# Row-maximum passes over 1,024 keys instead of 512 in the second and third block of an attention kernel

## The reference, cut to what matters

```python
def _L0_xattn_ref(image_features, text_features, Wq, bq, Wk, bk, Wv, bv):
    query = jnp.einsum('bqi,ih->bqh', image_features, Wq) + bq
    key = jnp.einsum('bkt,th->bkh', text_features, Wk) + bk
    value = jnp.einsum('bkt,th->bkh', text_features, Wv) + bv
    scale = 1.0 / jnp.sqrt(jnp.asarray(HID, query.dtype))
    scores = jnp.einsum('bqh,bkh->bqk', query, key) * scale
    weights = jax.nn.softmax(scores, axis=-1)
    return jnp.einsum('bqk,bkh->bqh', weights, value)
...
x = x + jnp.tanh(g_xattn[0]) * _L0_xattn_ref(_layernorm(x, axis=-1), ctx_768, ...)
x = x + jnp.tanh(g_ffn[0]) * _L0_ffn_ref(_layernorm(x, axis=-1), ...)
```

## Time and profile before

| | us |
|---|---|
| median of 3 runs (303.92 to 305.04) | 304.34 |
| the profiled execution | 305.22 |
| its span, from the first to the last instruction | 303.1 |
| PE busy | 289.5 (96%) |
| DVE busy | 220.0 (73%) |
| ACT busy | 211.3 (70%) |
| POOL busy | 81.7 (27%) |

### The profile page before, as it was taken

How to read it: one execution, slowest core, us unless ns; L and a number is a source line. 1 busy time by engine, 2 the same in 40 slices (tenths; PEclk the granted TensorE clock), 3 DMA queues, 4 the chain that set the end, 5 groups by cost and what they waited for, 6 DMA issues and landing times.

```text
span 303.1 us, 4501 instructions
## 1 busy us (share of the span) xinstructions
PE 289.5 (96%) x1577; PEld 252.3 (83%) x1577; DVE 220.0 (73%) x395; ACT 211.3 (70%) x333; POOL 81.7 (27%) x81
## 2 busy tenths in 40 slices
PE   6798899999999999999999989899999999999995
PEld 5565699999999999998999979888878878888883
DVE  4589699998598987995347478855868956756666
ACT  2678656666575665657677757669879889888881
POOL 5999940000000300000002944433141311111310
PEclk9889799999999999999999999999999999999999
DMA  7500400000000000000000252221011121121120
GB/s 209 211 0 3 138 1 3 0 2 0 2 0 2 1 0 2 0 0 4 0 0 2 69 139 71 73 67 71 32 39 35 41 68 35 42 99 36 37 67 35
DMA packets 10641, 12.40 MB, mean 41 GB/s; under 512 B 1530, under 2 KB 6524, under 8 KB 10620
## 3 DMA queue, kind: packets, MB, share of 16 engines
q1 hardware_dynamic: 10140, 11.90, 12.9%
q10 hardware_dynamic: 480, 0.23, 0.3%
HBM read 11.57 MB, written 0.56 MB: 40 GB/s over the span
## 4 chain that ended last, share of the span: by engine, by line
PE 87%; DVE 7%; POOL 2%; issue 2%; ACT 1%; DMA 1%; DVEq 0%; POOLq 0%; ACTq 0%
PE ps L872 8%; PE ps L873 8%; PE ps L893 8%; PE ps L808 8%; PE ps L874 8%; PE ps L895 8%; PE ps L894 8%; PE ps L939 5%; PE ps L941 5%; PE ps L940 5%; PE ps L967 4%; PE ps L968 4%; PE ps L966 4%; DVE pmax L584 3%; POOL norm L361 1%
## 5 line engine op out<-in xcount | busy, mean ns | idle before, releaser
L532 ACT ACTIVATE ex_hi<-ps 128x768 fp32r<-128x768 f32 (+1 forms) x78 | 57.0, 731 | 62.7 <-PE ps L874 62.1
L697 DVE TENSOR_TENSOR ex_lo<-ps,ex_hi 128x768 fp32r<-128x768 f32 (+1 forms) x78 | 66.4, 852 | 29.0 <-ACT ps L533 27.4
L584 DVE TENSOR_REDUCE pmax<-ps 128x1 f32<-128x512 f32 (+1 forms) x104 | 65.8, 666 | 11.5 <-PE ps L808 10.3
L738 DVE TENSOR_TENSOR ex_lo<-ps,ex_hi 128x512 fp32r<-128x512 f32 x64 | 44.0, 691 | 29.8 <-ACT ps L548 29.2
L533 ACT ACTIVATE ps<-ps 128x768 f32<-128x768 f32 (+1 forms) x78 | 56.5, 724 | 0.0
L872 PE MATMUL ps<-q_hi,ctxT_hi 97*128 97x384 f32 (+1 forms) x153 | 50.1, 327 | 2.9 <-DVE ex_lo L697 2.4
L547 ACT ACTIVATE ex_hi<-ps,cols 128x512 fp32r<-128x512 f32 x64 | 44.2, 691 | 11.6 <-PE ps L941 10.8
L893 PE MATMUL ps<-ex_hi,ctx_hi 128*97 128x384 f32 (+1 forms) x153 | 49.6, 324 | 0.0
L873 PE MATMUL ps<-q_lo,ctxT_hi 96*128 96x384 f32 (+1 forms) x153 | 49.5, 324 | 0.0
L874 PE MATMUL ps<-q_hi,ctxT_lo 96*128 96x384 f32 (+1 forms) x153 | 49.1, 321 | 0.0
L895 PE MATMUL ps<-ex_lo,ctx_hi 128*97 128x384 f32 (+1 forms) x153 | 48.7, 318 | 0.0
(11 more groups left out here) (117 smaller groups left out, 443.8 us busy)
## 6 DMA issues: line engine op xcount, KB each, us to landing
w_raw<-in_L_ffn_W_dram SPq DMA_DIRECT2D x16, 256.0 KB, 3.1
r_b<-routing SPq DMA_DIRECT2D x16, 256.0 KB, 3.2
raw<-in_ctx_dram SPq DMA_DIRECT2D x6, 384.0 KB, 6.1
tok<-in_x_dram SPq DMA_DIRECT2D x1, 384.0 KB, 4.3
out_dram<-norm SPq DMA_DIRECT2D x1, 256.0 KB, 2.5
tok<-in_x_dram SPq DMA_DIRECT2D x1, 128.0 KB, 2.3
out_dram<-norm SPq DMA_DIRECT2D x1, 128.0 KB, 1.7
out_dram<-norm ACTq DMA_DIRECT2D x1, 128.0 KB, 1.8
```

What stands on the lines that cost most here:

```text
L532: nc.scalar.activation(ex_pair(ex_hi, u % P_RING, js, n), scores, ACT.Exp)
L584: nc.vector.tensor_reduce(pmax[:, FIRST_TILE[b] + t, place:place + 1], MPAIR[:, s % 2, 0:w], AX.X, ALU.max).then_inc(max_reduced, 1)
L697: nc.vector.tensor_tensor(ex_pair(ex_lo, u % P_RING, js, n), whole, ex_pair(ex_hi, u % P_RING, js, n).bitcast(F32), ALU.subtract).then_inc ...
```

## The change

In blocks 1 and 2 one pass covers 1,024 keys. It is made of two matmuls of 512 columns, which fill both banks of `MPAIR`, and one reduction of DVE that reads both banks. A block then has 21 passes in place of 39: 3 tiles by 6 pieces of 1,024 keys, and 3 passes of 260 keys. Since a pass takes both banks, it waits for the reduction of the pass right before it. Block 0's own passes stay as they are. `finish_max` reads the 7 columns of `pmax` that are filled.

```diff
+    PASS = [BANK] + [2 * BANK] * (NB - 1)
+    PLACES = [-(-NKEY // p) for p in PASS]
+    SLOTS = [[(t, w * p, min(p, NKEY - w * p), w) for w in range(-(-NKEY // p)) for t in range(n)]
+             for n, p in zip(BLOCK_TILES, PASS)]
...
+        def max_home(b, s):
+            return flat(MPAIR) if b else MPAIR[:, s % 2, :]
...
-                nc.vector.tensor_reduce(pmax[:, FIRST_TILE[b] + t, place:place + 1], MPAIR[:, s % 2, 0:w], AX.X,
+                nc.vector.tensor_reduce(pmax[:, FIRST_TILE[b] + t, place:place + 1], max_home(b, s)[:, 0:w], AX.X,
...
-                if s >= 2:
+                if b and s >= 1:
+                    pe.wait_ge(max_reduced, SLOTS_BEFORE[b] + s)
+                elif s >= 2:
                     pe.wait_ge(max_reduced, SLOTS_BEFORE[b] + s - 1)
...
-                nc.tensor.matmul(MPAIR[:, s % 2, 0:w], q_hi[:, ft * P:(ft + 1) * P], ctxT_hi[0:CA, key:key + w],
-                                 start=True, stop=True).then_inc(max_scores, 1)
+                for at in range(0, w, BANK):
+                    n = min(BANK, w - at)
+                    last = nc.tensor.matmul(max_home(b, s)[:, at:at + n], q_hi[:, ft * P:(ft + 1) * P],
+                                            ctxT_hi[0:CA, key + at:key + at + n], start=True, stop=True)
+                last.then_inc(max_scores, 1)
```

More of the change, by code:

```diff
@@ L88, in attention_experts @@
     NMAX = -(-NKEY // BANK)
-    SLOTS = [[(t, w * BANK, min(BANK, NKEY - w * BANK), w) for w in range(NMAX) for t in range(n)]
-             for n in BLOCK_TILES]
+    PASS = [BANK] + [2 * BANK] * (NB - 1)
+    PLACES = [-(-NKEY // p) for p in PASS]
+    SLOTS = [[(t, w * p, min(p, NKEY - w * p), w) for w in range(-(-NKEY // p)) for t in range(n)]
+             for n, p in zip(BLOCK_TILES, PASS)]
     SLOTS_BEFORE = [sum(len(s) for s in SLOTS[:b]) for b in range(NB)]
@@ L588, in finish_max @@
                 dve.wait_ge(max_reduced, SLOTS_BEFORE[b] + len(SLOTS[b]))
-                nc.vector.tensor_reduce(nmax[:, tiles(b)], pmax[:, tiles(b), :], AX.X, ALU.max,
+                nc.vector.tensor_reduce(nmax[:, tiles(b)], pmax[:, tiles(b), 0:PLACES[b]], AX.X, ALU.max,
                                         negate=True).then_inc(nmax_ready, 1)
```

## The result

The changed kernel is slower. Its median is 310.36 us (310.07 to 312.79, 6 runs), and that of the kernel before in the same comparison is 307.20 us (303.92 to 311.42, 6 runs). The ratio of the two kernels is 1.0185 (95% interval 1.0141 to 1.0230). It counts only fast runs, those within 1.5% of the fastest of the same kernel, and so leaves out three of the kernel before (309.35, 309.80 and 311.42 us) and none of the changed one; the two medians of all runs are 3.2 us or 1.0% apart. In two later comparisons the same pair gave 1.0119 (1.0065 to 1.0173) and 1.0119 (1.0070 to 1.0167). Of its 25 runs in the three the lowest took 308.26 us. The lowest run of the kernel before in the whole study took 303.82 us.

A forecast was written before the change was run, and what follows sets the result against it. PE was taken to set the pace, with DVE just keeping up. In block 0 the loop's 3.6 us and the start's 0.5 made 4.1, on the median of 304.34 giving 308.4 us, range 306.0 to 310.9.

The forecast's parts named there:

- The loop: Block 0: each pair waits for the previous whole reduction, so units take 2.11 us against 1.90; 17 rounds cost 3.6 us.
- the wide reduction: On DVE: one reduction of 1,024 columns over two banks was to take 1.23 us.
- Rival (a): Block 0: DVE (VectorE) sets the pace and the edit relieves it, 1.1 us less, 303.2 us; chance 0.08.
- (b): Behind block 0: the loop's delay is given back later where PE has slack, 304.3 us; chance 0.07.
- Rival (c): Block 1: PE waits there too, eight units at 0.2 us, 1.6 us more, 310.0 us; chance 0.10.
- The steps of unit 7: Block 1: DVE's heaviest steps for block 0, 0.86 us, make the next reduction 0.35 us late against 0.40 of slack.
- from its end to PE's weight load: 0.11 us: Loop term in block 0: time from a reduction's end to the weight load that waited for it, 0.11 us.
- The start of block 0: First round, units 0 to 2: the pair of unit 2 starts 0.25 us later with one pass more to do, 0.5 us.
- Rival (d): The waits lower PE's clock; one stretch at 1.2 GHz would add 1 to 2 us, 310; chance 0.05.
- 91% busy: Against a clock fall: from 15 to 30 us PE is busy 13.7 of 15 us and its clock is 0.94.
- Block 1, forecast 0: Block 1: units of 2.58 us leave 0.40 us of slack, so PE doesn't wait and the cost is nothing.
- on the median of 304.34 I predict 308.4: Whole kernel: the 4.1 us added to the median of the kernel before, 304.34 us, gives 308.4 us.

The follow-up runs named there:

- e11: The changed kernel unaltered, measured a third time: ratio 1.0119 to the kernel before, lowest run 308.26 us.
- e1: The kernel before, unaltered, measured again: ratio 1.0025, lowest run 303.94 us.
- e16: The changed kernel with a second, idle wait placed ahead of the pair's wait for the reduction: ratio 1.0209 to the kernel before, lowest run 311.17 us.
- e18: The kernel before with eight extra idle matmuls around the turn of the maxima, just before block 0, and an added wait: ratio 1.0036, lowest run 304.97 us.
- e5: The kernel before, its 512-key passes in alternating banks placed as the changed kernel places its passes, none in unit 0: ratio 1.0019, lowest run 306.00 us.
- e14: As e5, with 20 extra idle matmuls and an added wait at the end of the opening stage: ratio 0.9969 to the kernel before, lowest run 303.80 us.
- e6: The changed kernel with its pairs and wait, but each bank read by its own reduction: ratio 1.0140 to the kernel before, lowest run 309.70 us.
- e13: The changed kernel with 20 extra idle matmuls and an added wait at the end of the opening stage: ratio 1.0062 to the kernel before, lowest 306.69 us.
- e15: The changed kernel with a second, idle wait written after the pair's wait for the reduction: ratio 1.0121 to the kernel before, lowest run 308.35 us.
- e8: The changed kernel with eight extra idle matmuls, two behind the passes of each of units 0 to 3 in block 0: ratio 1.0111, lowest 309.50 us.
- e9: The changed kernel with its wide passes begun one unit earlier, in units 0 to 20: ratio 1.0132 to the kernel before, lowest run 308.15 us.
- e7: The changed kernel with block 1's first six passes kept at 512 keys in alternating banks, then wide ones: ratio 1.0070, lowest run 306.99 us.

## Why the prediction came out as it did

**The mechanism was right.** Block 0 pays 4.0 of the 4.2 us by which e11's span is longer than e1's, and block 1 the rest. The loop is the one described, DVE is idle for 0.23 us in each unit (forecast about 0.2), and the wide reduction takes 1.224 us (forecast 1.23). Rival (a), that DVE sets the pace, is refuted: DVE's work fell and the time rose. So is (b): from block 2 on both kernels move in step, 4.59 us apart at its start and 4.65 at its end. Rival (c) did not happen as described. The steps of unit 7, put at 0.05 us from making PE wait, did not: that unit takes 2.58 us in both kernels, and the next, which has a pair now, 2.57 like its neighbours.

**The loop was mis-sized, 3.6 us forecast for its 17 rounds, 2.6 measured.** The step that failed is the handshake "from its end to PE's weight load: 0.11 us", which is 0.05. The earlier trace rows show a pass that has a separate semaphore instruction ahead of it for its wait, and the pass of block 0 is not of that form. The trace of before held both. Another reduction of the opening stage:

```profile
27.21 0.68 DVE L584 TENSOR_REDUCE pmax<-ps 128x1 f32<-128x512 f32 x1
```

It ends at 27.89, and this load follows:

```profile
27.95 0.19 PEld L808 LDWEIGHTS ps<-ctxT_hi,q_hi 97*128 97x128 f32 x1 [0.35 <-DVE pmax L584]
```

That is 0.05 us. The timeline names DVE as this load's releaser and "issue" as the one of the earlier trace rows. e16 shows that the form makes the difference: the same loop with a separate wait runs at the 2.11 us that I had forecast.

**The start of block 0 was mis-sized, 0.5 us forecast, 1.4 measured** (4.0 less 2.6). The step that failed took for granted that PE is back at 2.4 GHz from the pair of unit 2 on, as in the trace of before. Rival (d), the clock, had a chance of 0.05 and a wrong place: I looked for a fall of the clock in the loop, where it never fell. What happened is that the low clock that block 0 starts with lasts longer, 6.8 us instead of 3.4, which makes 1.0 of the 1.4. With it at bay 0.2 in unit 2 and 0.3 of the placement are left (the terms are rounded). My argument that 91% busy had kept the clock up in the opening stage looked at the wrong stretch. From 30 to 33 us PE is busy for 1.77, and e18 shows that this is where the fall of the clock is decided.

**Block 1, forecast 0, measured 0.25 us.** e5 has 0.15 of it without any loop and e14 0.20, and by the periods of the units it lies in units 1 and 2, which lose what unit 0 gains by having no pass. The likely reason, not tested, is that there `values` still runs over the narrow chunks of block 0, and units last near 2 us rather than 2.58. I had judged the block by its steady units.

**The two errors of the sum nearly cancelled** (4.1 forecast for block 0, 4.0 measured), which is no merit of the method.

**The level was wrong, and this is the step by which the forecast of the change missed most.** The step "on the median of 304.34 I predict 308.4" took three runs for the kernel's level. They were from the low end of what it does: with three more its median is 307.20 (303.92 to 311.42), and 308.4 is only 1.2 us above that. The change itself was measured as 5.7 us by the ratio, 3.2 by the medians, 4.7 by the two profiled spans and 3.7 by each later comparison (1.0119), around the 4.1 of the sum. That 310.36 lies inside the range of 306.0 to 310.9 is therefore luck in part: with the same sum, a level of 307.20 would have given 311.3. What makes the level move is the clock in part. Another part is the opening stage: it lasts 32.0 us in e1 and e11 and 33.2 and 33.4 in the first two traces, and why is open.

## What to carry to other kernels

Before two buffers in turn are merged into one wide read, add up the ring that this closes: read, handshake, fill, handshake. If that sum is longer than the period of the engine that sets the pace, the merge costs the difference in every round, however much it relieves the reader. Here the lost overlap costs 0.21 us a round (e6, 2.11 against 1.90) and the merged read saves 0.06 of it, so 0.15 is left to pay. The Trainium skill's rule on matmuls (Perfetto Trace Analysis, section Matmuls), to rotate through banks so that the reading of one overlaps the matmuls of the next, is borne out by e13 against e14 with 2.7 us. Take a handshake's price from a row in which the waiting instruction has the same form of wait. And take a kernel's level from more than three runs where they spread by more than the effect.

## What the runs showed of the hardware

- One reduction over 1,024 columns in two banks of PSUM takes 1.224 us, against 0.687 for 512 and 0.42 for 260. That is on the line through the two (1.23), so two banks in one read cost nothing extra.
- A wait on PE for DVE costs 0.05 us when the weight load carries it and 0.11 to 0.12 when it is a separate semaphore instruction. Which wait becomes the separate one follows the order in the code: the one written last did in e15 and e16. It costs nothing when it is for something long done (units of 2.05 us in e15, as without it).
- Eight idle matmuls of 256 columns in the last 2 us before block 0 kept PE at 2.4 GHz there in the trace of e18, and so did the twenty in four more traces. The mean granted clock from 32 to 42 us was 0.50 to 0.83 in all 15 traces without them. The same kind of fill inside block 0, after the clock had fallen, did nothing (e8, 6.8 us at 1.2 GHz). What exactly the chip asks of PE in order to stay at 2.4 GHz was not measured, and two things stay open: why the low stretch lasts 6.8 us in two traces of the changed kernel and 10.3 in a third, and why it is longer in e9 and in the trace of e7.
